# Decoder layer: the ternary FFN weights made during self attention and passed through device memory, and three steps of cross attention moved

## The reference, cut to what matters

```python
x = _layernorm(x + self_attention(x))                    # 16 heads of 128, rotary, signed softmax
x = _layernorm(x + cross_attention(x, ctx, mask))        # 16 heads of 32, clip(+-50), residual scale, gamma, beta
x = _layernorm(x + ffn(x))

def weight_quant(w):
    scale = 1.0 / jnp.clip(jnp.mean(jnp.abs(w)), 1e-5, None)
    return jnp.clip(jnp.round(w * scale), -1.0, 1.0) / scale      # ternary: -1, 0, 1
def bitlinear(x, w, b):                                           # used twice: w1 512->2048, w2 2048->512
    return jnp.einsum('bsd,fd->bsf', activation_quant(x), weight_quant(w)) + b
```

## Time and profile before

| | us |
|---|---|
| median of 3 runs | 1596.0 (1593.98 to 1597.33) |
| the profiled execution | 1593.35 |
| its span in the trace | 1591.5 |
| PE busy | 1432.8 (90% of the span) |
| DVE busy | 1271.7 (80%) |
| ACT busy | 807.9 (51%) |
| POOL busy | 713.5 (45%) |
| DMA moved | 52.46 MB, 33 GB/s on average |

### The profile page before, as it was taken

The page is one execution under the profiler, slowest core; times in us unless marked ns, Lnnn a source line. Parts: engine busy times, 40 slices in busy tenths (PEclk is TensorE's granted clock), DMA queues, the critical chain, the costliest instruction groups (busy, mean ns, idle before and its releaser), DMA issues.

```text
span 1591.5 us, 26282 instructions
## 1 busy us (share of the span) xinstructions
PE 1432.8 (90%) x8643; PEld 1136.7 (71%) x8660; DVE 1271.7 (80%) x2120; ACT 807.9 (51%) x1906; POOL 713.5 (45%) x765
## 2 busy tenths in 40 slices
PE   5999999999999999999999998888888885289997
PEld 5788888888888888888888886666666663134544
DVE  6988888888888888888888886367787789868885
ACT  4444444444444444444444434465555555578875
POOL 4334334334334334334334334445656655445554
PEclk9999999999999999999999999799999998589999
DMA  5300000000000000000000003200000005100001
GB/s 200 133 15 27 14 14 27 13 14 27 13 14 27 13 14 27 13 13 27 13 9 18 0 0 92 88 15 14 15 14 0 14 1 211 40 20 20 28 21 40
DMA packets 23541, 52.46 MB, mean 33 GB/s; under 512 B 3350, under 2 KB 3862, under 8 KB 22044
## 3 DMA queue, kind: packets, MB, share of 16 engines
q1 hardware_dynamic: 23452, 51.46, 9.7%
HBM read 47.25 MB, written 4.21 MB: 32 GB/s over the span
## 4 chain that ended last, share of the span: by engine, by line
PE 47%; DVE 29%; issue 11%; POOL 5%; ACT 5%; DMA 1%; DVEq 1%; SPq 0%; POOLq 0%; ACTq 0%
PE psum L269 9%; PE psum L271 8%; PE psum L270 8%; DVE rope_b L430 6%; PE psum L1451 3%; ACT xe L1161 3%; PE psum L1423 3%; DVE total_e L443 3%; PE psum L310 2%; DVE acc L473 2%; DVE p L439 2%; DVE s L411 2%; PE psum L1440 2%; PE psum L331 2%; DVE rope_a L430 2%
## 5 line engine op out<-in xcount | busy, mean ns | idle before, releaser
L610 POOL TENSOR_TENSOR qk<-rope_a,rope_b 128x512 f32<-128x512 f32 x128 | 177.0, 1382 | 570.1 <-DVE rope_b L430 570.1
L269 PE MATMUL psum<-x_hi,w_hi 128*128 128x512 f32 x512 | 210.5, 411 | 10.3 <-POOL w_lo L604 10.3
L517 ACT ACTIVATE e<-s 128x384 f32<-128x384 f32 x128 | 66.4, 519 | 281.6 <-DVE s L411 281.6
L271 PE MATMUL psum<-x_hi,w_lo 128*128 128x512 f32 x512 | 201.7, 394 | 0.0
L270 PE MATMUL psum<-x_lo,w_hi 128*128 128x512 f32 x512 | 201.6, 394 | 0.0
L430 DVE SCALAR_TENSOR_TENSOR rope_b<-psum,qk_bias,sin 64x512 f32<-64x512 f32 x256 | 192.0, 750 | 3.7
L1161 ACT ACTIVATE xe<-xe,mask_now 128x256 f32<-128x256 f32 x256 | 131.7, 590 | 98.5 <-DVE xe L961 98.5
L411 DVE SCALAR_TENSOR_TENSOR s<-psum,tri 128x384 f32<-128x384 f32 x128 | 70.7, 553 | 121.3 <-PE psum L310 121.3
L269 PE MATMUL psum<-w_hi,x_hi 128*128 128x256 f32 x512 | 147.4, 288 | 0.0
L270 PE MATMUL psum<-w_lo,x_hi 128*128 128x256 f32 x512 | 144.7, 283 | 0.0
L271 PE MATMUL psum<-w_hi,x_lo 128*128 128x256 f32 x512 | 144.6, 282 | 0.0
(11 more groups left out here) (192 smaller groups left out, 3949.2 us busy)
## 6 DMA issues: line engine op xcount, KB each, us to landing
stage<-w_self_dram SPq DMA_DIRECT2D x64, 256.0 KB, 2.8
raw<-w_dram SPq DMA_DIRECT2D x6, 1024.0 KB, 11.0
acc<-xT_dram SPq DMA_DIRECT2D x4, 1024.0 KB, 7.8
acc<-x_dram SPq DMA_DIRECT2D x1, 4096.0 KB, 14.9
c_raw<-ctxT_dram SPq DMA_DIRECT2D x8, 512.0 KB, 3.3
xstage<-w_cross_dram SPq DMA_DIRECT2D x16, 256.0 KB, 3.1
out_dram<-yb SPq DMA_DIRECT2D x16, 256.0 KB, 2.0
raw_last<-w_dram SPq DMA_DIRECT2D x2, 1024.0 KB, 15.0
```

Of the source, the lines that this page charges most:

```text
L269: pe.matmul(ps, ah, bh, start=n == 0, stop=False)
L271: last = pe.matmul(ps, al, bh, start=False, stop=n == len(pairs) - 1)
L517: nc.scalar.activation(e[:, b, :], s[:, b, :], ACT.Abs)
L610: nc.gpsimd.tensor_tensor(qk[:, k % 2, which, :], rope_a[:, which, :], rope_b[:, which, :], ALU.add).then_inc(qk_ready, 1)
```

## The change

The sums, the scale and the ternary form of w1 and w2 move into self attention. The weights lie in one tensor `w_ffn` of 16 pieces of 128 x 1024. Over the loop passes 0 to 3 ACT takes the sum of absolute values of a piece in the slots k = 6, 1, 2, 3; pass 4 folds them and makes the scale; then ACT makes one piece per slot ternary (shift, then sign) in slots k = 2, 3 of pass 4, k = 5, 6, 1, 2, 3, 4 of passes 5 and 6, and two of the last slots. SP keeps each piece as bf16 in an internal tensor `w_signs` in device memory, and loads both weights from there (2 MB each) late in cross attention, with gamma, beta and b2 behind them. For this the loop of the other engines is cut into 4 passes, one written out, and 2 passes; ACT's slots and SP's piece loads are all written out. In cross attention PE turns x behind `mix`, DVE's `take_x` follows `norm`, ACT's `take_q(1)` comes before the second half of `exps` in step 3, `round_c` one step earlier, and POOL's `split_c` before `sum_e` in step 3.

```diff
@@ self_attention: slots
-            with eng.Fori(0, GROUPS - 1) as i:
+            with eng.Fori(0, SCALED_IN) as i:                       # SCALED_IN = 4
                 for j in range(LAG, LAG + 8):
                     emit(i * 8 + j, j % 8, i)
+            for j in range(LAG, LAG + 8):
+                emit(SCALED_IN * 8 + j, j % 8, SCALED_IN)
+            with eng.Fori(SCALED_IN + 1, GROUPS - 1) as i:
...
@@ self_attention: sync
+            def load_raw(q, buf):
+                sp.dma_start(w_raw[:, buf, :], T["w_ffn"][q]).then_inc(raw_in[buf], 16)
+            def keep_signs(q):
+                sp.wait_ge(w_signed, q + 1)
+                sp.dma_start(w_signs[q], w_sign[:]).then_inc(w_kept, 16)
+            load_raw(0, 0)
+            load_raw(1, 1)
+            for g in range(1, GROUPS):
+                load_group(g, range(4))
+                if g - 1 > SCALED_IN:
+                    for r in range(2):
+                        q = (g - 2 - SCALED_IN) * 6 + r + 2
+                        keep_signs(q)
+                        load_raw(q + 2, r)
+                load_group(g, range(4, PIECES))
+                if g - 1 < SCALED_IN:
+                    for q in range(4 * g - 4, 4 * g):
+                        sp.wait_ge(w_totalled, q + 1)
+                        load_raw((q + 2) % W_PIECES, q % 2)
...
@@ self_attention: tensor, vector
+            def total_weights():                                    # PE, pass 4, end of slot k = 7
+                pe.wait_ge(w_folded, 2)
+                pe.wait_ge(w_consts, 1)
+                pe.matmul(psT[:, LW:LW + 2], ones[:], w_sum[:], start=True, stop=True).then_inc(w_meant, 1)
...
+                if isinstance(t, int) and i == SCALED_IN and k == 0:
+                    pe.wait_ge(w_meaned, 1)                         # before turn(t - 2, 0)
...
+            def fold_weights():                                     # DVE, pass 4, end of slot k = 6
+            def scale_weights():                                    # DVE, pass 4, start of slot k = 0
...
@@ self_attention: scalar, behind totals in a slot
+            def total_piece(q):
+                act.wait_ge(raw_in[q % 2], (q // 2 + 1) * 16)
+                nc.scalar.activation(w_sign[:], w_raw[:, q % 2, :], ACT.Abs, accum_out=w_part[:, q:q + 1]
+                                     ).then_inc(w_totalled, 1)
+            def sign_piece(q):
...
+                act.wait_ge(raw_in[q % 2], (W_PIECES // 2 + q // 2 + 1) * 16)
+                nc.scalar.activation(raw, raw, ACT.Identity, scale=w_inv[:, of:of + 1], bias=rnd[:]
+                                     ).then_inc(w_shifted, 1)
+                act.wait_ge(w_shifted, q + 1)
+                wait(act, w_kept, q * 16)
+                nc.scalar.activation(w_sign[:], raw, ACT.Sign, bias=nrnd[:]).then_inc(w_signed, 1)
...
-            slots(act, emit)
+            for t in range(UNITS + LAG):
+                emit(t, t % 8, (t - LAG) // 8 if LAG <= t < UNITS - 8 + LAG else None)
@@ cross_attention: tensor
+                    pb, pc = before(b, i)
+                    if live(pb):
+                        mix(pb, par if i else 1 - par, pc)
                     if i == 2 and live(b + 1):
                         turn_x(b + 1, 0)
                         turn_x(b + 1, 1)
-                    pb, pc = before(b, i)
-                    if live(pb):
-                        mix(pb, par if i else 1 - par, pc)
@@ cross_attention: vector (take_x moved from before the w_lo pieces and norm to behind norm)
-                    if isinstance(b, int):
-                        ahead["vector"](dve, b, i)
@@ cross_attention: scalar
+                    if i == 3 and live(nb):
+                        take_q(nb, npar, 1)
                     if live(b):
                         exps(b, par, i, (2, 3))
-                    if i == 3 and live(nb):
-                        take_q(nb, npar, 1)
...
-                    if i == 3 and live(b + 2):
+                    if i == 2 and live(b + 2):
                         if not (isinstance(b, int) and b + 2 == 0):
                             round_c(b + 2)
@@ cross_attention: gpsimd (split_c of step 3 moved from behind sum_e and split_o to before sum_e)
@@ feed_forward
+            sp.wait_ge(sems["w_kept"], w_signs.shape[0] * 16)
+            for n, w in enumerate((w1, w2)):
+                sp.dma_start(w[:].rearrange("p a b -> p (a b)").rearrange("p (n k) -> p n k", n=half),
+                             w_signs[n * half:(n + 1) * half].rearrange("n p k -> p n k")).then_inc(w_in[n], 16)
+            for dst, src in ((gamma, "gamma1"), (beta, "beta1"), (b2, "b2")):
+                sp.dma_start(dst[:], T[src].partition_broadcast(P)).then_inc(small_in[src], 16)
...
-            for c in range(4):
-                sign_weight(c)
```

More of the change, by code:

```diff
@@ L195, in self_attention @@
         b1_split = sem("b1_split")
+        w_raw = sb("w_raw", [P, 2, W_COLS])
+        w_sign = sb("w_sign", [P, W_COLS], BF16)
+        raw_in = [sem(f"raw_in{i}") for i in range(2)]
+        w_consts = sem("w_consts")
+        w_totalled = sem("w_totalled")
+        w_folded = sem("w_folded")
+        w_meant = sem("w_meant")
+        w_meaned = sem("w_meaned")
+        w_inverted = sem("w_inverted")
+        w_shifted = sem("w_shifted")
+        w_signed = sem("w_signed")
+        env["shared_sems"]["w_kept"] = w_kept = sem("w_kept")
         b1 = sb("b1", [P, 3, F // P])
@@ L258, in sync, with load_group @@
             sp.dma_start(acc[:], T["x"].rearrange("b (j p) d -> p (b j) d", p=P)).then_inc(acc_in, 16)
-            with sp.Fori(1, GROUPS) as g:
-                for n in range(PIECES):
+            def load_group(g, pieces):
+                for n in pieces:
                     sp.wait_ge(w_ready, g * PIECES + (n - STG + 1))
                     sp.dma_start(stage[:, n % STG, :], T["w_self"][g, n]).then_inc(stage_in[n % STG], 16)
+            def load_raw(q, buf):
[17 more added lines that the diff above has]
+                        load_raw((q + 2) % W_PIECES, q % 2)
+                elif g - 1 == SCALED_IN:
+                    for q in range(2):
+                        keep_signs(q)
+                        load_raw(q + 2, q % 2)
+                else:
+                    for r in range(2, 6):
+                        q = (g - 2 - SCALED_IN) * 6 + r + 2
+                        keep_signs(q)
+                        load_raw(q + 2, q % 2)
+            for q in range(W_PIECES - 2, W_PIECES):
+                keep_signs(q)
         def tensor(pe):
@@ L380, in emit @@
                     output(t, k, 1)
+                if isinstance(t, int) and i == SCALED_IN and k == 7:
+                    total_weights()
             slots(pe, emit)
@@ L476, in emit @@
                 odd = k % 2 == 1
+                if isinstance(t, int) and i == SCALED_IN and k == 0:
+                    scale_weights()
                 if live(t, 1):
@@ L503, in emit @@
                     split_x(t + 1)
+                if isinstance(t, int) and i == SCALED_IN and k == 6:
+                    fold_weights()
             slots(dve, emit)
@@ L1089, in emit @@
                         norm(pb, pc)
+                    if i == 2 and live(b + 1):
+                        take_x(b + 1, 0)
+                        take_x(b + 1, 1)
                     if i == 0:
@@ L1267, in emit @@
                         root(2, b - 2, (x2_ready, (b - 2) * 2))
+                    if i == 3 and live(b + 2):
+                        if not (isinstance(b, int) and b + 2 == 0):
+                            split_c(b + 2)
                     if live(b):
@@ L1282, in emit @@
                             root(1, b - 1, (scaled, b - 1))
-                    if i == 3:
-                        if live(b + 2):
-                            if not (isinstance(b, int) and b + 2 == 0):
-                                split_c(b + 2)
             bodies(pool, emit)
@@ L1370, in load_weights @@
             sp.wait_ge(sems["wo_ready"], CH)
[L1371 to L1377 removed]
+            half = w_signs.shape[0] // 2
+            sp.wait_ge(sems["w_kept"], w_signs.shape[0] * 16)
[4 more added lines that the diff above has]
+                sp.dma_start(dst[:], T[src].partition_broadcast(P)).then_inc(small_in[src], 16)
         def sync(sp):
[L1380 to L1382 removed]
             for t in range(TILES):
@@ L1387, in sync @@
                 sp.wait_ge(done, TILES // 2 * 16)
-        def total_weight(pe, n):
-            if n == 0:
-                pe.wait_ge(env["shared_sems"]["kq_out"], B * 8)
-            pe.wait_ge(s["w_folded"], n + 1)
-            pe.matmul(psW[n][:, 0:1], ones[:], w_sum[:, n:n + 1], start=True, stop=True).then_inc(s["w_meant"], 1)
         def tensor(pe):
@@ L1500, in abs_sum_2 @@
-        def abs_sum_2(act, c):
-            act.wait_ge(w_in[1][c], 16)
-            flat = w1[:].rearrange("p a b -> p (a b)")
-            nc.scalar.activation(flat[:, c * QUARTER:(c + 1) * QUARTER], w_raw[1][c], ACT.Abs,
```

(11 more changed lines are left out.)

162 lines of the change are left out of this document (58 added, 104 removed).

## The result

The changed kernel takes 1568.0 us in the median (1565.5 to 1568.8, four runs) against 1596.4 (1594.0 to 1597.3) of the kernel before beside it: ratio 0.982, interval 0.9805 to 0.9839. Forecast were 1564.4 us and 1552 to 1579. The profiled execution had 1567.6 around a span of 1565.8, so 25.7 us of span are to be found.

What follows compares the result with a forecast made beforehand. PE was taken to bound self attention, and a chain from engine to engine cross attention. Terms 0 - 4.7 - 11.3 - 10.4 - 5.2 = -31.6 from the median 1596.0 gave 1564.4 us, range 1552 to 1579.

Steps and rivals of the forecast that it cites:

- Self attention, 0: Self attention: ACT's added 54 us of weight work fits its idle time, so slots stay at 14.95 us; 0.
- A: Rival: self attention's slots grow by 0.5 us in all 32, +16, giving 1580.4 us; chance 0.09.
- C: Rival: SP's queue makes ACT cast late and PE stop, one slot in each of 7 groups, 105 us: 1669; chance 0.04.
- First images, -4.7: Cross attention's fill and images 0 and 1: context and query waits go, `take_x` costs about 1.3: -1.5, -1.0 and -2.2.
- Images 2 to 6, -11.3: Cross attention, five images: period falls from an average of 42.99 to 40.73 us, -2.26 an image.
- The turn of the earlier trace: Cross attention: one 43.79 us chain from DVE clip to clip loses waits of 0.82, 0.57 and 1.67, leaving 40.73.
- neither the late query nor c_lo holds PE: Cross attention, images 2 to 6: the reason given why ACT's 1.67 us wait for the keys goes.
- Rival D: Cross attention's chain shortens more, with POOL's `finish_y` earlier and PE's clock full: up to 9 us more, 1555; chance 0.09.
- End of cross attention, -10.4: Up to the first FFN tile, DVE loses its FFN weight work: -2.2, -4.4 and -3.8.
- The third is on DVE's own path: End of cross attention: DVE's third weight sum, 2.28 us, lies on its path to the clip of step 3: -2.2.
- Start of the FFN, -5.2: First GELU starts 6.35 us behind PE's L1399 instead of 11.6; -3.9 if the table load isn't hidden.
- -5.2 + 2.66: Start of the FFN, by the Trainium skill's table-switch cost with nothing hidden: -2.6 instead of -5.2.

Runs made afterwards that it cites:

- double_act: Changed kernel with 48 more absolute-value passes of 128 x 1024 on ACT in self attention, into a buffer nobody reads: 1569.4 us.
- c_undone: Changed kernel with the context's rounding (`round_c`) back in step 3 and `split_c` back behind `sum_e` and `split_o` of step 3: 1582.3 us.
- x_undone: Changed kernel with PE turning the next image's x before `mix` and DVE's `take_x` before `norm` again: 1569.7 us.
- pool_reorder: Changed kernel with POOL finishing tile 0 in step 0, then the root, and tile 1 in step 1 behind the sum of e: 1552.5 us.
- moves_only: Kernel before with only the six moves in cross attention; weights still made ternary at cross attention's end: 1581.1 us.
- takex_first: Changed kernel with only DVE's `take_x` put before `norm` again: 1571.6 us.
- best: pool_reorder with both tiles of the last image finished by DVE and one raw weight piece loaded later in self attention: 1553.4 us.
- q_undone: Changed kernel with ACT's `take_q(1)` of step 3 behind the exponentials again: 1573.3 us.
- pool_takex: pool_reorder with DVE's `take_x` put before `norm`: 1554.0 us.

## Why the prediction was right, and where not

**Self attention, 0: right.** 940.96 / 63 = 14.94 us a slot, ACT +51.3 us (54 forecast), its pause before the next scores 3.20 where it was 3.53; double_act shows the room behind it. Rivals A and C did not occur. The first score of image 0 is 0.15 us later: a slot k = 0, 15.45 us in the earlier trace rows, now takes 15.03 to 15.12, for a reason not sought, and the late slot at the end of this document takes 1.2 back.

**First images, -4.7: -4.5 by the ledger, -4.4 with what lies before them; right in size, wrong in its parts.** I gave the waits for c the 2.85 us of the earlier trace rows, and took 1.3 off an image for `take_x`. Undone, c costs 6.2 us in these two images and x gains 4.6; both were about twice what I had for them, and they cancel. Over these two images PE waits 13.6 us in c_undone, 8.7 in the changed kernel and 6.6 in x_undone, and its work takes 68.2, 66.9 and 64.4 us at a clock of 0.92, 0.93 and 0.98. c's effect is mostly waiting, which counts in full, as the prediction had it; more than half of x's reaches PE as a higher clock, for which the sum had no term.

**Images 2 to 6, -11.3: -10.1, 40.97 us an image against 40.73. The average is near, and partly by luck.** No image had that period: from first score to first score they took 39.16, 42.44, 41.99, 42.48 and 38.76 us, where the kernel before has 42.58, 43.77, 43.48, 42.72 and 42.38. The turn of the earlier trace rows went from 43.79 to 41.85, 1.94 less and not 3.06. Its second part, from the clip in step 0 to the one behind x1_norm, gave 1.61 where 1.67 was forecast: ACT no longer waits for the keys there. Its first part gave 0.33 in place of 1.39. Both waits in it went, but `c_lo`, moved, runs on POOL from 1173.09 to 1175.48, just when DVE copies the mask. The copy before and after:

```profile
1179.97 0.15 DVE L955 COPY mask_now<-mask 128x4 f32 x1
```

```profile
1173.08 2.43 DVE L1073 COPY mask_now<-mask 128x4 f32 x1
```

In c_undone it is 0.15 or 0.16 in every image. The sum had no term for what a moved pass of POOL does to DVE beside it. Two things made up for this. The sum set the new turn of one long image against the average of all five, 2.26 less and not 3.06; and images 2 and 6 lost about 3.5 us each. In those two `scale_y` takes 1.00 us, in images 3 to 5 3.06 to 3.09 beside POOL's sum of e; that this parts them is not tested.

The step "neither the late query nor c_lo holds PE" held for c, but q still makes PE wait 1.4 us in two images and x 4.9 us over five, where the signs had under 1 and none. It also did not say which move carries the gain: singly undone, c is worth 7.0 here, x 4.7 and q 2.4, together more than the 10.1, so they are no terms of a sum. The new wait for `x_lo` of about 2 us came as forecast, five times. Rival D, a clock that stays full and POOL's `finish_y` earlier, is in part what happened to the clock (0.94 to 0.98).

**End of cross attention, -10.4: -8.0.** The cuts and `floor_weight` went as computed: 4.3 before `finish_last` (4.4 forecast) and 3.7 behind it (3.8); the steps up to the first `take_y` gave 1.0 that I had not counted. Two terms were mis-sized. "The third is on DVE's own path" was not so: `take_y` then waited for PE's output, and only 0.66 of 2.2 us came:

```profile
1324.90 0.69 DVE L1140 TENSOR_TENSOR y<-psum,ob 128x512 f32<-128x512 f32 x1 [1.34 <-PE psum L936]
```

And the cuts had kept DVE away from POOL: without them both engines do the same kind of pass at once, and the three rows shown above take 4.8 us, in the kernel before 1.75 + 0.69 + 0.69 = 3.1. These 1.7 us were missing from the sum, though the trace of before has POOL's three passes beside the cuts of the earlier trace rows, slowed like them.

**Start of the FFN, -5.2: -3.2.** ACT's timeline:

```profile
1374.15 1.28 ACT L1681 ACT_TABLE_LOAD   x1
1377.81 1.11 ACT L1681 ACTIVATE h<-psum,xd 128x1024 f32<-128x1024 f32 x1 [2.37 <-PE psum L1519]
...
1380.38 1.11 ACT L1681 ACTIVATE h<-psum,xd 128x1024 f32<-128x1024 f32 x1 [1.37 <-PE psum L1519]
```

The table load is hidden and the first GELU starts 6.38 us behind the turn at 1371.43 (6.35 forecast). But its second half now waits 1.37 us for PE, where it used to find its input ready: of an early start only what the next in line can follow is gained. That is 1.4 of the 2.0 us that are missing; the other 0.6 is not traced. (The prediction's -5.2 + 2.66 is -2.54 and not -2.6; the load is hidden, so neither that case nor its -3.9 came.)

The terms fell short by 0.3, 1.2, 2.4 and 2.0 us: 25.7 in place of 31.6. The median is 3.6 and not 5.9 above the forecast, because the profiled execution of before lay 2.65 under its median and this one 0.4.

## What to carry to other kernels

The total of the waits under a name is not what that name is worth: where three producers are late for one consumer, moving the two with the most waiting uncovered the third, the smallest; undone alone it costs 13 us where all the moves together gave 15. Undo the moves one at a time to price them, and split the span by marks that every version has: a move can gain in one part what it loses in another, as x did. Look at each part's busy time and granted clock beside its waits, and at what a pass that is moved will run beside. An average that comes out as forecast doesn't show that its parts did. When waits remain, look at the engine they name (here POOL, 45% busy) for an order that answers the nearest consumer first; it was worth about as much as all the moves.

## What the runs showed of the hardware

**DVE and POOL slow each other.** A DVE pass over 128 x 512 with two inputs takes 0.69 us alone and 1.56 to 1.63 beside POOL's passes, and these 1.50 to 1.59 instead of 1.28. Some one-input passes suffer too: `scale_y`, two passes, is 1.00 us in the last image and 3.06 at 1185.70, beside POOL's sum of e, and the mask's copy of 128 x 4 grew from 0.15 to 2.43. Passes that read PSUM kept their time: `take_y` at 1197.80 takes 0.69 us beside the same kind of sum. So DVE's busy time is no property of its own work: for the same instructions in images 2 to 6 it was 171.3 us before, 180.7 after, 163.5 in c_undone and 185.2 in pool_reorder, the fastest. My lower bound of 34.3 us an image, DVE's own work, rested on it. The Trainium skill (SBUF — State Buffer, SBUF: two separate sides) calls the port pair that the two share an exclusive lock that the loser waits for. The slower passes here agree with that. But the six passes, which alone are 5.9 us, were done 5.4 us after the first began, so in the records they overlap in part.

**A late slot.** Wherever the weights' pieces are moved in self attention, except in double_act, the slot that begins at 800 to 802 us took 15.9 to 18.4 us (16.12 in the changed kernel). At its beginning DVE starts on the scores after an idle time of 3.6 to 4.4 us (2.5 in double_act, and in moves_only, which has no such transfers), in four kernels with nothing named that it waited for, as in takex_first:

```profile
804.28 0.56 DVE L494 SCALAR_TENSOR_TENSOR s<-psum,tri 128x384 f32<-128x384 f32 x1 [4.19 <-issue]
```

Packets of the instruction queues run there while 1.75 MB of pieces and signs keep the DMA engines busy. It looks like instructions fetched late behind that traffic; best took 0.5 MB of it away and changed little, so this stays open. In q_undone, x_undone and takex_first it took 18.2 to 18.4 us, which is some 2 of the 2 to 4 us that their profiles lie behind the changed kernel's before cross attention begins, and is why they are judged by the ledger.

Not tried: `take_x` before `norm` in images 0 and 1 alone, which x_undone puts at some 4 us for the changed kernel and pool_takex at 1.2 for pool_reorder.
